# The order of instructions on five engines, written anew in one kernel of gated cross-attention and mixture of experts

## What is computed

```python
x = x + tanh(g_xattn) * xattn(layernorm(x), ctx)   # softmax(Q K^T / sqrt(32)) V, then Wo; biases on all four
n = layernorm(x)
probs = softmax(n @ router_w + router_b)           # 8 experts
gate, idx = max(probs), argmax(probs)
x = x + tanh(g_ffn) * gate * (n @ expert_w[idx] + expert_b[idx])
```

## Time and profile before

| | |
|---|---|
| device time, median of 3 runs | 1189.92 us (1188.95 to 1192.12) |
| the profiled execution | 1192.07 us, span of the trace 1190.3 |
| TensorE busy | 1094.6 us, 92% |
| VectorE busy | 759.0 us, 64% |
| ScalarE busy | 563.0 us, 47% |
| GpSimd busy | 667.2 us, 56% |
| TensorE's granted clock, mean | 0.956 of 2.4 GHz |

### The profile page before, as it was taken

The page is one execution under the profiler, slowest core; times in us unless marked ns, Lnnn a source line. Parts: engine busy times, 40 slices in busy tenths (PEclk is TensorE's granted clock), DMA queues, the critical chain, the costliest instruction groups (busy, mean ns, idle before and its releaser), DMA issues.

```text
span 1190.3 us, 19122 instructions
## 1 busy us (share of the span) xinstructions
PE 1094.6 (92%) x5464; PEld 709.2 (60%) x5464; DVE 759.0 (64%) x1620; ACT 563.0 (47%) x1016; POOL 667.2 (56%) x446
## 2 busy tenths in 40 slices
PE   2798999999999999999999999999999996898996
PEld 1564467556755675567556655575557642786774
DVE  4645545766576657665765677556765665778654
ACT  4145643564356435644564356445644456423431
POOL 3046645764576457645764576545764555644662
PEclk9798999999999999999999999899999986699998
DMA  6233323423343334333332342233332319324541
GB/s 230 62 77 102 82 72 80 113 80 81 79 121 80 81 77 119 82 79 89 111 79 72 79 120 72 73 80 111 86 81 73 83 53 321 127 95 147 166 140 54
DMA packets 70885, 119.39 MB, mean 100 GB/s; under 512 B 17854, under 2 KB 18878, under 8 KB 70656
## 3 DMA queue, kind: packets, MB, share of 16 engines
q1 hardware_dynamic: 62496, 98.96, 30.2%
q0 software_dynamic: 6240, 18.68, 5.0%
q10 hardware_dynamic: 2048, 0.53, 0.2%
HBM read 50.42 MB, written 18.66 MB: 58 GB/s over the span
## 4 chain that ended last, share of the span: by engine, by line
PE 68%; DVE 13%; issue 6%; ACT 5%; POOL 3%; DMA 3%; DVEq 1%; ACTq 0%; SPq 0%; POOLq 0%
PE jb L459 10%; PE jb L460 9%; PE jb L461 9%; PE sc L482 8%; PE jb L502 8%; PE hb L492 8%; DVE maxima L836 6%; PE sc L664 5%; ACT probs L688 3%; PE jb L602 2%; PE jb L515 2%; POOL psum_keys L1095 2%; PE jb L530 1%; PE jb L594 1%; PE hb L650 1%
## 5 line engine op out<-in xcount | busy, mean ns | idle before, releaser
L836 DVE TENSOR_REDUCE maxima<-jb 128x1 f32<-128x512 f32 x512 | 321.7, 680 | 112.2 <-PE jb L502 110.8
L688 ACT ACTIVATE probs<-sc 128x512 f32<-128x512 f32 x512 | 285.4, 598 | 190.5 <-PE sc L482 153.8
L1095 POOL TENSOR_TENSOR psum_keys<-psum_keys,probs 128x1024 f32<-128x1024 f32 x128 | 302.6, 2384 | 110.7 <-ACT probs L688 110.6
L1095 POOL TENSOR_TENSOR psum_keys<-probs 128x1024 f32<-128x1024 f32 x64 | 151.8, 2383 | 231.3 <-ACT probs L688 230.9
L502 PE MATMUL jb<-k_stack,q_stack 96*128 96x512 f32 x512 | 188.4, 435 | 19.1 <-issue 4.9
L482 PE MATMUL sc<-q_stack,k_stack 98*128 98x512 f32 x512 | 190.7, 435 | 14.9 <-ACT probs L688 11.5
L482 PEld LDWEIGHTS sc<-q_stack,k_stack 98*128 98x128 f32 x512 | 94.4, 192 | 107.6 <-ACT probs L688 56.0
L502 PEld LDWEIGHTS jb<-k_stack,q_stack 96*128 96x128 f32 x512 | 92.6, 190 | 110.4 <-issue 51.2
L492 PE MATMUL hb<-probs,values 128*32 128x512 f32 x1024 | 139.3, 628 | 3.4 <-ACT probs L688 2.5
L459 PE MATMUL jb<-c_hi,wk_hi 128*128 128x512 f32 x128 | 52.4, 409 | 15.4 <-POOL c_lo L1099 15.4
L664 PE MATMUL sc<-e_hi,heads_hi 128*128 x156 | 65.9, 422 | 0.5 <-DVE heads_raw L1067 0.5
(11 more groups left out here) (226 smaller groups left out, 1958.6 us busy)
## 6 DMA issues: line engine op xcount, KB each, us to landing
k_stack<-k_hi SPq DMA_DIRECT2D x256, 64.0 KB, 2.0
q_stack<-q_hi SPq DMA_DIRECT2D x256, 64.0 KB, 2.0
stage<-in_x SPq DMA_DIRECT2D x63, 256.0 KB, 2.9
stage<-in_ctx_t SPq DMA_DIRECT2D x32, 256.0 KB, 3.0
k_stack<-k_lo SPq DMA_DIRECT2D x128, 64.0 KB, 2.0
q_stack<-q_lo SPq DMA_DIRECT2D x128, 64.0 KB, 2.0
e_lo<-in_ew SPq DMA_DIRECT2D x8, 1024.0 KB, 14.0
rows<-row SPq DMA_DIRECT2D x30, 257.5 KB, 3.0
```

The costliest lines, as they stand in the source:

```text
L688: nc.scalar.activation(probs[:, kt % 2, h, :], scs[(16 * g + n) % NSC][:], ACT.Exp, scale=SCALE)\
L836: nc.vector.tensor_reduce(maxima[g % 2][:, n:n + 1], jbs[j][:], AX.X, ALU.max).then_inc(s["mx_done"], 1)
L1095: nc.gpsimd.tensor_tensor(psum_keys[:, two, :], in0, probs[:, kt % 2, two, :], ALU.add)\
```

## The change

Only the tables `OPENING`, `ORDER` and `CLOSING` change; items are put in another order, and a few move from one body to the next (`1MT`, `~LR1`, the row load `DR1`, and on GpSimd the part from `OP0` on, which now stands at the head of the next body). No item is added or taken away, and no other line of the kernel changes. The new file has one more line in the tables, so each line number below them is one higher. The core of the diff, with the list of ScalarE in the opening, two lines of its list in the steady batch and GpSimd's list there:

```diff
 ORDER = {
...
     "ACT": [
...
-        "~RT3 2E15 3MT 3MD ~RS1 ^0K 2OU 3E0 3E1 3E2 3E3 3E4 2SUM 3E5 3E6 3E7 3E8 3E9 2SC 3E10 3E11 3E12 3E13 2NM",
...
+        "2E14 ~RT3 3MT 3MD 2E15 ~RS1 ^0K 3E0 3E1 3E2 3E3 3E4 3E5 3E6 2OU 3E7 2SUM 2SC 3E8 3E9 3E10 3E11 3E12 3E13",
...
     "POOL": [
-        "~LR0 1A0 ^C0 1A1 ^C1 ^C2 ^C3 1A2 ~OP2 ~OP3 1A3 1A4 1A5 ~LR1 ^LX0 ^LX1 2A0 2A1 ^LX2 ^LX3 2A2 2A3 2A4 2A5",
-        "OP0 OP1 3A0 3A1 3A2 3A3 3A4 3A5 ^0A0 ^0A1 ^0A2 ^0A3 ^0A4 GA0 ^0A5",
+        "~OP0 ~~LR1 ~2A4 ~2A5 ~3A0 ~3A1 ~3A2 ~3A3 ~3A4 ~3A5 0A0 0A1 0A2 0A3 0A4 ~OP1 ~LR0 0A5 1A0 ^C0 1A1 ^C1 ^C2",
+        "1A2 1A3 ~OP2 ^C3 ~OP3 1A4 1A5 ^LX0 ^LX1 2A0 2A1 ^LX2 ^LX3 2A2 2A3",
     ],
 }
 
 OPENING = {
...
     "ACT": [
-        "WT0 WT1 WT2 WT3 ^C0 ^C1 TH WT4 ^C2 WT5 ^C3 ^0K ^NX0 WT6 WT7 WT8 WT9 ^T4 WT10 ^NX1 WT11 WT12 ^NX2 ^T5 ^NX3",
...
+        "^C0 ^C1 WT0 WT1 ^C2 ^C3 WT2 WT3 TH WT4 ^NX0 ^NX1 WT5 WT6 WT7 WT8 WT9 WT10 WT11 ^0K ^T4 ^NX2 ^NX3 ^T5 ^T6",
```

More of the change, by code:

```diff
@@ L50 @@
     "SP": [
-        "~~RW2 1SQ 1SK ^DC0 ~~RW3 2SQ 2SK ^DC1 ^DC2 ~RW0 ~RW1 ^DC3 ~DR2 ~DR3 ^DX0 3SQ ^DX1 3SK ^DX2 ^DX3 DR0 DR1",
+        "~~RW2 ~DR1 ~~RW3 1SQ 1SK 2SQ ^DC0 2SK ^DC1 ^DC2 ^DC3 ~RW0 ~RW1 ~DR2 ~DR3 3SQ ^DX0 ^DX1 3SK ^DX2 ^DX3 DR0",
         "^0SQ ^0SK",
@@ L90 @@
     "SP": [
-        "LW1 ^DC0 ^DC1 ^DC2 LW0 ^DC3 ^DX0 LC LW2 LW3 ^DX1 ^DX2 ^DX3 ^0SK ~RW2 ~RW3 ^0SQ",
+        "^DC0 ^DC1 LW1 ^DC2 ^DC3 ^DX0 LW0 ^DX1 LC ^DX2 LW2 ^DX3 LW3 ~RW2 ^0SK ~RW3 ^0SQ",
     ],
     "PE": [
[5 rows of a table removed]
[5 rows of a table added]
     ],
     "ACT": [
[3 rows of a table removed]
[4 rows of a table added]
     ],
     "DVE": [
[4 rows of a table removed]
[3 rows of a table added]
     ],
     "POOL": [
-        "^C0 ^C1 ^C2 ^C3 ^LX0 ^LX1 ^LX2 ^LX3 ^0A0 ^0A1 ^0A2 ^0A3 ^0A4 ^0A5",
+        "^C0 ^C1 ^C2 ^C3 ^LX0 ^LX1 ^LX2 ^LX3",
     ],
@@ L117 @@
     "SP": [
-        "~~RW2 ~DR2 W0 ~~RW3 W1 W6 W2 W3 W4 W5 W7 ~DR3 EB ~RW0 ~RW1 ~RW2 ~RW3",
+        "~DR1 ~~RW2 ~~RW3 ~DR2 W0 W1 W6 W2 W3 W4 W5 W7 ~DR3 EB ~RW0 ~RW1 ~RW2 ~RW3",
     ],
```

## The result

The changed kernel takes 1200.0 us (median of 4 runs, 1198.14 to 1201.75) against 1189.43 for the kernel before: ratio 1.0085, 95% interval 1.0062 to 1.0109. It is slower where 1175.5 was forecast. On another chip the same pair gave 1.0052 [1.0032, 1.0071]. The attention part is no slower there: one and the same batch of the kernel after takes 120.50 us here and 120.52 there. From the first second-round score of the last batch to the end it takes 302.5 us here and 316.6 there. So all experiments are given as ratios to the kernel before, run beside them, and traces are compared in the attention part alone. One execution of 5643.53 us, of the kernel before with the gate on GpSimd, was in the slow state and is in no ratio.

A forecast was written before the change was run, and what follows sets the result against it. TensorE, 68% of the chain of waits, was taken as the bound, gains possible only where it waits or runs at lower clock. -5.5 -1 -9.8 +1.5 = -14.8 us from 1189.92 gave 1175.1, stated as 1175.5; range 1167 to 1188.

The forecast's parts named there:

- the third: Steady batch, VectorE: RC, K and RG together ahead of M4; RG some 1.2 us, M4 to M15 at most 1.3 us earlier.
- rival B: Steady batches: the new order weakens a place, the clock falls, five batches pay 4.34 us each, so 1197; chance 0.10.
- such a pair: VectorE's two-number instruction ending as GpSimd's run of sums ends: where the two newly meet, up to 1.4 us cost.
- the opening: Before the steady batches: earlier C conversions and x load put Q at 27.8; -5.5 us, bounds -3 and -8.
- the rest of the steady batch: Gains on TensorE, ScalarE, VectorE and GpSimd overlap along one chain: -1.4 us per batch (-0.5 to -2.5), over seven intervals -9.8.
- Q's start: Steady batch, TensorE: with items moved past it, Q starts about 1.4 us earlier and M0 1.3 to 1.5 earlier.
- OU's place: Steady batch, ScalarE: OU, the copy of the heads, moves behind the seventh exponential; the first exponential starts 0.5 us earlier.
- S14 and S15: Steady batch, TensorE: these two scores go before Q, one of the moves behind M0's 1.3 to 1.5 us gain.
- 1 us for 2K: Batch 0: one M of group 2 waits 2.1 us for k_stack; an earlier 2K gives back 1 us.
- The closing: Last group to first output projection: sums earlier, but W1, W6 and the early plan ahead of NM; +1.5 us (-1 to +3.5).

The follow-up runs named there:

- the gate on GpSimd: Last instruction of RG (gate times tanh, two numbers a lane) done by GpSimd, not VectorE: 1.0045 of before on the kernel before, 0.9962 of before on the kernel after.
- the filled wait: Kernel after with score S10 of group 1 put ahead of M8 on TensorE and its matmul issued nine times: 0.9985 of the kernel before.
- P1 in the wait: Kernel after with the gate's multiplication on GpSimd, and P1 and S10 of group 1 ahead of M8 on TensorE: 0.9930 of the kernel before.
- VectorE's piece alone: Kernel before with only VectorE's RC0, K of group 3 and RG0 in a row ahead of M4 and M5: 1.0169 of the kernel before.

## Why the prediction was wrong, by its steps

**The step that failed** is the third: "three small instructions of RG (some 1.2 us with what they wait) ahead of the reductions", M4 to M15 "can't end more than 1.3 us earlier". From RC's start to M4's reduction lay 3.50 us before (452.20 to 455.70); it is 6.44 now, and RG alone takes 2.26 of it (338.46 to 340.72), not 1.2. RC does start 2.4 us earlier, counted from the batch's S0, but M4's reduction starts 0.5 later (50.7 us behind S0 in place of 50.1), while TensorE comes to M7 3.7 us earlier (48.9 behind S0 in place of 52.6), with four banks and nothing else in its list but M. TensorE's M15 then comes 2.2 us later than before (59.4 behind S0 in place of 57.1). I priced the list of VectorE and never asked at which M TensorE would run out of banks: 2.22 us of wait, and about as much again behind it, on which the forecast had nothing outside rival B.

**A price was in hand and not used.** The prediction read the instruction of 1.60 us that ends with GpSimd's sums, and said "where such a pair newly meets, it costs up to 1.4". It didn't look for where, and its 1.4 was too low. RG0 is such an instruction; GpSimd's sum A1 runs at its new place; it costs 1.96 - 0.23 = 1.73 us on the path to M4. Moving that instruction to GpSimd is worth 0.9% of the kernel.

**Rival B was what happened**, at another place than it named. It was given 0.10, with 4.34 us for each batch hit. The place is M8 of group 2, not the transposes; all six steady batches are hit; the clock's part is 2 us a batch by the filled wait, so B's price was twice too high. That its 1197 is near 1200.0 is luck: the wait itself, and the gains of the opening that batch 0 gave back, make up for the price.

**What was right: the rest of the steady batch.** With the gate on GpSimd a batch at full clock takes 117.59 (283.72 to 401.31), and with P1 in the wait 117.55, against 118.70: -1.15, where -1.4 was forecast (-0.5 to -2.5). Batches of these kernels that took up to 119.0 at full clock are left out of this figure; what held them isn't known. So the new order earns most of what I counted, and loses it and 1.8 us more at one wait. That split is shown by the kernels with the wait filled and the gate moved; how much of the 1.15 is Q's start, OU's place or S14 and S15 was not taken apart.

**The opening** gave 3.65 at S0 in place of 5.5. The waits of K for c_lo are gone, but waits of 0.66 and 1.01 us for the low part of its weights take their place, and its last step begins at 18.12, where 14.6 to 16.3 was forecast (19.98 before). T6 then had to wait longer (TensorE's timeline):

```profile
27.59 1.97 PE L588 MATMUL jb<-ident,stage 128*128 128x128 f32 x8 [6.14 <-ACT stage L726]
```

ScalarE's timeline has the reason:

```profile
23.59 2.19 ACT L741 ACTIVATE wv_hi<-psum_keys 128x512 fp32r<-128x512 f32 x4 [2.52 <-DMA psum_keys<-in_wv_t]
```

ScalarE's normalization of the third tile, at 26.73, stands behind four conversions of Wv, which wait 2.52 us for their load. So Q began at 30.97, not 27.8. I had followed the items that moved forward and not the twelve that now stand ahead. Batch 0 then gives the gain back (106.47 against 102.64): its waits are 1.55 for the sums and 1.72 ahead of P3 of group 2, among others. Of the 1 us for 2K 0.6 came (M0 of group 2 waits 0.50 in place of 1.10), and was worth nothing at the batch's end.

**The closing** costs 1.5 behind the first projection (181.85 against 180.38), the size forecast, and that is luck: the 1.5 was forecast ahead of the first projection. From the first score of group 3 of the last batch to the first projection it takes 31.96 us after and 32.67 before. What makes the 1.5 behind it, in one trace of each kernel, was not looked into.

## What to carry to other kernels

When the order of one engine is changed, ask of each engine that it feeds how many buffers it has, at which item it runs out of them, and what else it could do then; here two microseconds with nothing to do cost about as much again in the clock behind them. A tiny instruction may carry the largest price: look at where another engine's long run lies beside it, and at which queues wait for its result. Two orders that were made together (here TensorE's and VectorE's) can't be judged or taken back one list at a time.

## What the runs showed of the hardware

A VectorE multiplication of two numbers in each lane takes 0.23 us with GpSimd idle, and 1.47, 1.96 and 4.33 us beside GpSimd's key sums, each time until one of these ends. The 4.33 spans two sums of 2.4 us back to back: it did not get in between them, in all six batches of that kernel. But it isn't always so. In the kernel after the 1.96 ends with the sum at 340.78, though GpSimd's next instruction begins at 340.74, and in the kernel before with VectorE's piece alone the first of two such instructions of the layer norm ends between two sums, at 360.8, and the next is held over the second sum:

```profile
359.46 1.38 DVE L915 TENSOR_SCALAR rt<-st 128x2 f32<-128x2 f32 x1
360.76 2.38 DVE L916 TENSOR_SCALAR rt<-st 128x2 f32<-128x2 f32 x1
```

What decides between the two is not shown. The reduction and the reciprocal just ahead of the gate's multiplication, 0.15 to 0.17 us, are not held.
